# Value products in pairs, one wait per PSUM bank around the gated layer, and a later turned input tile, in a fused attention and feed-forward kernel

## The reference

```python
def attn(x, qkv_w, out_w):                      # x is layer-normed first
    q, k, v = split((x @ qkv_w.T))               # 16 heads of 16
    q = q * cos + rotate_half(q) * sin           # the same for k
    scores = einsum('bhqd,bhkd->bhqk', q, k) * scale
    scores = where(mask, scores, finfo.min)      # causal, and same block, |i-j| <= 128, or j < 4
    out = einsum('bhqk,bhkd->bhqd', softmax(scores), v)
    return out @ out_w.T

def ffn(x, ...):                                 # x is layer-normed first
    h = silu(x @ w1.T * s1) * (x @ w2.T * s2)    # 256 -> 1024, "gated"
    h = gelu(h @ h1.T * sh1)                     # 1024 -> 1024
    h = gelu(h @ h2.T * sh2)                     # 1024 -> 1024
    return h @ w3.T * s3                         # 1024 -> 256

x = x + attn(layernorm(x), ...)
x = x + ffn(layernorm(x), ...)
```

## Time and profile before

| | us |
|---|---|
| median of 3 runs | 1191.78 (1191.38 to 1192.52) |
| the profiled execution, its own time | 1194.19 |
| its span, first to last instruction | 1192.3 |
| TensorE matmul busy | 1091.3 (92%) |
| VectorE / ScalarE / GpSimd busy | 649.3 / 715.3 / 472.2 |

### The profile page before, as it was taken

The page is one execution under the profiler, slowest core; times in us unless marked ns, Lnnn a source line. Parts: engine busy times, 40 slices in busy tenths (PEclk is TensorE's granted clock), DMA queues, the critical chain, the costliest instruction groups (busy, mean ns, idle before and its releaser), DMA issues.

```text
span 1192.3 us, 21621 instructions
## 1 busy us (share of the span) xinstructions
PE 1091.3 (92%) x7538; PEld 877.2 (74%) x7538; DVE 649.3 (54%) x1986; ACT 715.3 (60%) x1774; POOL 472.2 (40%) x656
## 2 busy tenths in 40 slices
PE   4175869999999999999999999999999999999998
PEld 2144667778867787778877788777877778778887
DVE  3078535754566545755566555765557554554422
ACT  1445545765666844855657745857657756866422
POOL 6243142722543433723535323634427223323433
PEclk9678989999999999999999999999999999999999
DMA  9777745776447344555537364465446464431540
GB/s 300 234 195 251 222 147 171 243 234 178 150 130 233 111 155 160 179 175 148 180 109 243 101 195 148 151 198 158 133 136 213 122 193 152 117 107 54 177 141 18
DMA packets 138269, 198.54 MB, mean 167 GB/s; under 512 B 7856, under 2 KB 90032, under 8 KB 138160
## 3 DMA queue, kind: packets, MB, share of 16 engines
q1 hardware_dynamic: 138160, 197.14, 53.8%
HBM read 155.16 MB, written 49.28 MB: 171 GB/s over the span
## 4 chain that ended last, share of the span: by engine, by line
PE 83%; SPq 4%; DVE 4%; DMA 3%; ACT 2%; issue 2%; POOL 1%; POOLq 0%; ACTq 0%; DVEq 0%
PE bank L708 39%; PE bank L679 10%; PE bank L732 5%; PE bank L618 5%; PE bank L575 5%; PE bank L587 4%; PE bank L516 4%; PE bank L595 3%; PE bank L540 2%; PE bank L641 2%; SPq L370 2%; SPq L330 1%; DMA qk_scratch<-split 1%; DMA Qs<-qk_scratch 1%; PE bank L631 1%
## 5 line engine op out<-in xcount | busy, mean ns | idle before, releaser
L851 ACT ACTIVATE Sm<-Sm,smin 128x260 f32<-128x260 f32 (+2 forms) x512 | 241.4, 473 | 211.4 <-DVE smin L1033 210.9
L708 PE MATMUL bank<-b_hi,W 128*128 128x512 f32 x512 | 216.5, 423 | 0.5 <-POOL b_lo L1284 0.5
L708 PE MATMUL bank<-a_hi,W 128*128 128x512 f32 x512 | 210.4, 411 | 1.1 <-DVE a_act L1120 1.1
L708 PE MATMUL bank<-b_lo,W 128*128 128x512 f32 x512 | 201.3, 393 | 0.0
L708 PE MATMUL bank<-a_lo,W 128*128 128x512 f32 x512 | 201.0, 392 | 0.0
L1084 DVE TENSOR_SCALAR a_sum<-bank,scales 128x512 f32<-128x512 f32 x64 | 48.0, 751 | 159.4 <-PE bank L708 159.4
L679 PE MATMUL bank<-x_hi,W 128*128 128x256 f32 x512 | 127.0, 289 | 7.6 <-issue 7.6
L1293 POOL TENSOR_TENSOR a_lo<-a_act,a_hi 128x256 fp32r<-128x256 f32 x128 | 94.2, 738 | 83.5 <-ACT a_hi L898 83.5
L679 PE MATMUL bank<-x_lo,W 128*128 128x256 f32 x512 | 125.4, 286 | 0.0
L575 PE MATMUL bank<-Ks,Qs 128*128 128x256 f32 (+1 forms) x512 | 100.3, 319 | 19.9 <-DVE a_act L1120 8.2
L1033 DVE CUSTOM_DVE_ANT_0 Sm<-bank,msk,gmin 128x256 f32<-128x256 f32 x256 | 108.4, 480 | 11.3 <-PE bank L575 11.3
(11 more groups left out here) (110 smaller groups left out, 2188.2 us busy)
## 6 DMA issues: line engine op xcount, KB each, us to landing
W<-w_scratch SPq DMA_DIRECT2D x168, 512.0 KB, 4.0
qk_scratch<-split SPq DMA_DIRECT2D x128, 256.0 KB
Qs<-qk_scratch SPq DMA_DIRECT2D x128, 128.0 KB, 4.7
Ks<-qk_scratch SPq DMA_DIRECT2D x16, 1024.0 KB, 8.5
w_scratch<-in_ffn_w SPq DMA_DIRECT2D x22, 512.0 KB, 8.1
stage_a<-in_ffn_w SPq DMA_DIRECT2D x16, 512.0 KB, 8.5
x_in<-in_x SPq DMA_DIRECT2D x8, 512.0 KB, 9.2
x<-in_x SPq DMA_DIRECT2D x8, 512.0 KB, 4.0
```

The source lines that it names most:

```text
L708: mm = nc.tensor.matmul(bank[n % 2][:, :], lhsT.bitcast(F32) if general else lhsT, rhs, start=(kk == 0 and part == 0), stop=(kk == NH - 1 ...
L851: ex = nc.scalar.activation(row, row, ACT.Exp, bias=smin[:, r, c:c + 1], scale=-1.0, accum_out=rowsum[:, i % 2, col:col + 1])
```

## The change

The diff, whole. The semaphore counts in it: `GATED` is 16, `mul_done` counts products of the gated layer, so `GATED * a - 2` is reached with the product of tile 13, the last in bank 3, and `GATED * (r + 1) - 1 + n` with that of tile 14 for n = 0 (bank 0) and tile 15 for n = 1 (bank 1).

```diff
@@ scores @@
                 elif a:
-                    pe.wait_ge(mul_done, GATED * a)
+                    pe.wait_ge(mul_done, GATED * a - 2)
@@ deep_quarter @@
                 if quarter == 0:
-                    if n == 0:
-                        pe.wait_ge(mul_done, GATED * (r + 1))
-                    elif n >= 2:
+                    if n < 2:
+                        pe.wait_ge(mul_done, GATED * (r + 1) - 1 + n)
+                    else:
                         pe.wait_ge(sum_kept, DEEP * r + n - 1)
@@ step @@
-                t, u = n - T_LAG, n - PV_LAG
+                t = n - T_LAG
...
-                if with_a and n == UNITS:
-                    ln2_transposes(r, 0)
                 if with_a and n == UNITS + 1:
                     turn_globals(r, 1)
                 if with_f and n < DEEP:
                     deep_quarter(r, n, 2, general)
-                if with_a and 0 <= u < UNITS:
-                    weighted_values(a, u)
+                if with_a and n % 2 == 0:
+                    for u in (n - PV_LAG - 1, n - PV_LAG):
+                        if 0 <= u < UNITS:
+                            weighted_values(a, u)
+                if with_a and n == UNITS:
+                    ln2_transposes(r, 0)
@@ rounds (TensorE) @@
-                        if s == 3:
+                        if s == 5:
                             ln2_transposes(r - 1, NT - 1)
@@ gated (ScalarE) @@
-                    if s == 2:
+                    if s == 4:
                         keep_x2hi(r, NT - 1)
```

## The result

| | before | after |
|---|---|---|
| median, us | 1191.99 (1191.38 to 1192.52, 4 runs) | 1175.26 (1174.98 to 1175.56, 4 runs) |
| ratio after to before | | 0.9852, 95% interval 0.9841 to 0.9864 |
| the profiled execution, its own time | 1194.19 | 1174.98 |
| its span | 1192.3 | 1173.2 |
| mean granted clock | 0.971 | 0.966 |

The kernel became 16.7 us faster; 24.3 were forecast, and 1175.26 lies within the range of 1160 to 1180. Between the two profiled executions it is 19.2 us, because that of before lay 2.2 above its median and that of after did not.

What follows compares the result with a forecast made beforehand. TensorE's own list plus its waits was taken to bound each round. Savings 9.3 + 1.0 + 7.8 + 16.4 less losses 7.2 and 3.0 made 24.3 us: 1169.9 profiled, 1167.5 us median, range 1160 to 1180.

Steps and rivals of the forecast that it cites:

- 1. banks: scores, first deep block: Behind the gated layer, first scores and first deep matmul need earlier products: 9.3 us and 1.0 us saved.
- 2. tile 3: Turning of x2's tile 3, placed two tiles later: 1.11 us saved in 7 rounds, 7.8 us.
- 3. pairs, TensorE's side: Attention steps: each merged pair of value-product units saves 0.34 us; 2.34 a round, 16.4 us in 7 rounds.
- 4. wait for the keys: Step 8, rounds 0 to 5: global scores newly wait 1.2 us for `Kg`, 7.2 us lost.
- round -1: No quarters between the pieces, so the copies' new waits delay its end: 3.0 us lost, bounds 0 and 5.
- the pairs save nothing: Rival: on TensorE the 0.34 us belongs to each unit's first product, 16.4 is lost: 1184 us, chance 0.10.
- 0.68 + 0.30 = 0.98: Saving per round: 0.68 us through steps 12 to 16, 0.30 us by the pair of step 18.
- followed through steps 13, 14 and 15: Working that had ScalarE, GpSimd and TensorE's last-layer `a_lo` matmul come 0.68 us earlier, not 3 x 0.34.
- T + 3.2: Step 8: T is the start of the pair; TensorE starts the global scores 3.2 us after it.
- The short price of `split_lo`: Step 8, VectorE: `split_lo` taken as 0.62 us, wait 7.2 us in all; the long 1.63 gives 13.2.
- the carried delay: Round -1: new waits of about 0.9 us each in steps 12 and 14, carried on to the turning at 139.2.
- The base: Profiled execution's own time 1194.19 us; the runs' median is 2.4 below it, and the forecast median keeps that distance.

Runs made afterwards that it cites:

- the run with the keys first: The changed kernel with `global_keys` moved ahead of `keep_cur` on VectorE in step 8: 1165.63 us (ratio 0.9767).
- three places: The changed kernel with three places in `PT` instead of two, the room taken from `featT`: 1162.56 us (ratio 0.9745).
- the order behind them is mended: The changed kernel with the pair ahead of quarter 2, keys ahead of the copy, single units in round -1, two `PT` places: 1157.87 us (0.9710).
- the longer tail: The changed kernel with three 128x256 copies put on VectorE ahead of the global keys, step 8, rounds 0 to 5: 1188.45 us (ratio 0.9963).

## Why the prediction was right, and where not

Against the profiled execution 24.3 were forecast and 19.2 measured. By the steps of the forecast:

| term | forecast | measured |
|---|---|---|
| 1. banks: scores, first deep block | -10.3 | -10.9 |
| 2. tile 3 | -7.8 | -8.0 |
| 3. pairs, TensorE's side | -16.4 | -12.7 |
| 4. wait for the keys | +7.2 | +7.2 |
| round -1 | +3.0 | +5.5 |
| lower clock in round 4 | none | +1.6 |
| gated layer of round 0 | none | -1.2 |
| before's wait for `b_lo`, rounds 0 and 2 | none | -0.7 |

The measured terms are sums of the stage table over the rounds. Term 1 is 10.3 at the two waits and 0.6 in step 0 of the seven rounds; that step is as much shorter in the runs with the banks and no pairs, and not in that of the pairs alone. 3 and 4 are parted by the run with the keys first: the wait is 3.33 - 2.14 = 1.2 in each of six rounds. Rounds 0 and 2 come out at +0.61 in steps 7 and 8, and not at +0.98, since before's own step 8 was 0.4 longer there: its global scores started 2.03 after the products in place of 1.60, behind the wait for `b_lo` that the earlier trace rows do not show.

**1 and 2, right.** Both were read from one gap each and counted in full, since nothing behind them was late, and both are found again on the chip (10.5 and 8.0 by the ratios). The gated layer of round 0 is not part 2's: before's wait for tile 3 was only 0.2 there. Its first microseconds run at a granted clock of 0.50, for 5.6 us in before and 3.6 in after, so some 1.0 of the 1.2 is the clock (half of the difference). Over the profiles with the later tile 3 this low stretch lasted 3.0 to 6.0 us, and this layer came out between -1.4 and -0.1.

**3, the mechanism right, one term too large.** In steps 4, 6 and 10 a pair gives 0.32 to 0.35 (forecast 0.34), in step 8 only 0.25 (round 6, where no global scores are in the way), and two units in a row stand 0.46 apart. By the rule quoted from the Trainium skill ("TensorEngine Tiling (Array Packing)", Key Properties), that the change of tiling mode drains TensorE, and not that of the tile alone, this is what had to come; the trace agrees, and the rival *the pairs save nothing* is out. From step 11 to the end of the round 0.68 + 0.30 = 0.98 were forecast and 0.27 - 0.02 + 0.39 - 0.06 = 0.58 came (51.44 - 50.84 = 0.60 in round 2). The step of the working that failed is "followed through steps 13, 14 and 15". The late `keep_prev(10)` was seen, 0.63 against "about 0.6", and followed to the gelu and to GpSimd. Not followed was what else stands behind that gelu: `keep_prev(11)`, and through its bank `turn_prev(12)` on TensorE in step 14. So TensorE waits there until it is back at before's pace, the scores of step 15 come 0.25 earlier and not 0.66, and with them the last gelu and `a_lo`: 0.25, not 0.68. At the last layer's start TensorE is 0.64 ahead and then stands 0.22 for `a_lo`, which takes what the pair of step 18 saves. With the pair a quarter earlier the copies are on time, `a_lo` comes 0.65 earlier and the next gated layer 1.00: there the forecast's 0.68 and 0.98 are met. The term was too large by 0.4 in 7 rounds, 2.8 us; step 8 is another 0.1 a round.

**4, right in place and in size**: 1.2 in each of six rounds, T + 3.34 against T + 3.2. The short price of `split_lo` held. The Trainium skill ("SBUF — State Buffer", Who interferes with whom) has a VectorE operation with two SBUF inputs and a GpSimd operation that reads SBUF exclude each other. With GpSimd done 0.33 us before, nothing stood in the way and it took 0.66; the trace agrees. The wait disappears with the keys in front, shrinks by 0.91 with the pair 0.93 earlier and grows by 1.0 with 0.94 of copies in front: its cause is VectorE's order.

**Round -1, mis-sized.** `turn_cur(14)` starts 1.79 later than before, and 2 x 0.9 was forecast for the carried delay. That the two agree is partly luck: 0.75 of it stands already at the round's first scores, ahead of any pair. Then VectorE's copies, and TensorE:

```profile
135.12 0.68 DVE L1052 COPY PT<-bank 128x512 f32<-128x512 f32 x1
139.47 0.69 DVE L1052 COPY PT<-bank 128x512 f32<-128x512 f32 x1 [3.67 <-PE bank L618]
```

```profile
137.84 0.66 PE L595 MATMUL bank<-consts,Sm 128*128 128x128 f32 x4 [1.27 <-ACT PT L862]
138.43 0.93 PE L618 MATMUL bank<-PT,v_even 128*32 128x128 f32 x16
...
140.55 0.69 PE L650 MATMUL bank<-consts,xn 128*128 128x128 f32 x2 [0.34 <-DVE x L1068]
```

Before, the copy of 134.83 needed only `turn_cur(14)`. Now it needs the first unit of the pair, the pair stands on TensorE behind `turn_prev(14)`, and that waits 1.27 for ScalarE's copy behind its exponentials. So VectorE has inherited ScalarE's lateness, and the turning comes at 140.55, not at 139.2. Without quarters between the pieces, a group moved behind another is moved behind all that it waits for. The forecast bounded the loss by 0 and 5; it is 5.5 here, and single units in this round bring back 6.1.

This stretch scatters. Up to the first gated matmul the kernels with single units in round -1 come out from 3.0 shorter to 1.9 longer than before's profile; those with pairs and two places 5.3 to 6.8 longer, but for the pairs alone (-0.7). A narrower piece parts them cleanly: from the first scores of step 14 to TensorE's last matmul of round -1 (149.08 in before) it is 22.1 to 22.9 us in all seven profiles with single units, 24.5 to 26.6 in all six with pairs and two places, and 24.7 with three places. Up to that piece the profiles of one order differ by 2 to 3 us among themselves, and behind it TensorE runs nothing for 5.2 to 8.8 us until the first gated matmul, which is 1.1 of the 5.5 in after (8.8 against 7.7). The profile shows nothing that this last gap waits for. So that the pairs lose time here is shown; it is 2 to 4 us in this piece, and about 6 by the medians.

**The clock, not foreseen.** 1.6 us in round 4 of after's profile, none in that of its repetition.

**The base.** The forecast carried the distance of before's profile to its median, 2.4, over to the new kernel. After's profile lies on its median. With the 0.3 on after's side that is 2.7 of the 7.8 us by which the forecast was low, and the reason why 19.2 by the profiles is 16.7 by the medians; the repetition gives 17.5 (0.9853). So 10.5 us went against the forecast (pairs 3.7, round -1 2.5, the clock in round 4 1.6, the base 2.7) and 2.7 in its favour, of which it had named nothing: the clock and the rest of round 0's gated layer, before's waits for `b_lo`, step 0. That part is luck.

The pairs as a whole were to bring 16.4 - 7.2 - 3.0 = 6.2 and brought nothing: 12.7 on TensorE's side went to the keys (7.2) and to round -1 (5.5 or more). Alone they are at 1.0017, and with or without them the change stands at 0.9853 and 0.9845. It is faster by parts 1 and 2, and the pairs pay only once the order behind them is mended: 0.9710 against 0.9845, 16 us, near the 16.4 that TensorE's side was counted at, and 4.87 - 2.55 = 2.3 in the usual round, where the forecast had 2.34.

## What to carry to other kernels

When work is moved later so that two pieces merge, list every copy that waits for it, on each engine, then what is queued behind each copy, and also who else waits for the same bank; a wait of 0.2 us in the list can stand for a whole saving that never arrives. Put the merged work as early in the step as its inputs allow, and take what doesn't need the copy (here the keys) out from behind it: two places and a better order did as well as a third place. A stage without cover, like the first round here, should keep the old order.

## What the runs showed of the hardware

TensorE's granted clock can fall to half in the middle of full work. Between the start of round 0, whose first 3 to 6 us run at half, and the end of the last round it did so only behind the wait for the keys. Round 4 of after, TensorE, then the windows:

```profile
766.97 0.40 PE L709 MATMUL bank<-b_lo,W 128*128 128x512 f32 x1
768.40 1.05 PE L527 MATMUL bank<-Kg,q 128*128 128x32 f32 x8 [1.03 <-DVE Kg L996]
...
770.46 0.63 PE L709 MATMUL bank<-b_hi,W 128*128 128x512 f32 x1
770.89 0.63 PE L709 MATMUL bank<-b_lo,W 128*128 128x512 f32 x1
```

```profile
768.70:771.00 2.30, 2.30 (x15) 2.06 (x15) 1.69 (x8) 0.40 (x1) 1.54 (x3) 0.81 0.90 268
771.00:774.00 3.00, 3.00 (x13) 2.41 (x12) 1.56 (x6) 2.09 (x8) 0.62 (x3) 0.58 0.80 257
774.00:780.00 6.00, 6.00 (x35) 4.99 (x33) 2.36 (x9) 1.98 (x6) 0.45 (x3) 1.00 0.92 313
```

The deep matmuls, 0.23 apart at the full 2.4 GHz, stand 0.43 apart for some 3 us, which is the 1.2 GHz level, and then the clock is back; it costs 1.6 us. The engine had idled 1.03, worked for 2 us, and slowed after that. It happened in one of six rounds of after, none of its repetition, one with the pairs alone, two with round -1 single, and four of six with the longer tail (idle up to 2.0); in no profile in which the wait for the keys was gone or only 0.1 long. But the idle time alone isn't the cause: before stands 1.18 idle ahead of its scores in seven rounds at full clock, the kernel with three places, keys first and single units stands 1.07 idle in step 8 of round 1 (for `b_lo`) at full clock, and five waits of 1.03 to 1.05 in the repetition of after left the clock alone. What else decides was not tried.
